# First attention: key blocks of 128 from the first context row on, and a last block of 64 keys for the upper 64 queries

## The reference, cut to what matters

```python
k_full = jnp.concatenate([k_ctx, k], axis=1)
v_full = jnp.concatenate([v_ctx, v], axis=1)
...
causal = jnp.where(j > i, -jnp.inf, 0.0).astype(x.dtype)
mask = jnp.concatenate([jnp.zeros((L, T), x.dtype), causal], axis=1)
scores = jnp.einsum('blhd,bmhd->bhlm', q, k_full) * scale + mask
probs = jax.nn.softmax(scores, axis=-1)
out = jnp.einsum('bhlm,bmhd->blhd', probs, v_full)
...
return out @ wo
```

## Time and profile before

| what | value |
|---|---|
| median of 3 runs | 1954.93 us (1954.01 to 1955.39) |
| span of the profiled execution, first to last instruction | 1951.5 us |
| PE busy | 1834.0 us, 94% |
| DVE busy | 1096.8 us, 56% |
| ACT busy | 1036.9 us, 53% |
| POOL busy | 960.0 us, 49% |
| mean TensorE clock granted | 0.985 of full |

### The profile page before, as it was taken

One profiled execution on the slowest core, in us unless ns is written; L12 is line 12 of the kernel. 1 busy time (PEld: TensorE's weight loads), 2 busy tenths in 40 slices (PEclk: granted clock), 3 DMA queues, 4 the chain that ended last, 5 costly groups with the idle time before them and its releaser, 6 DMA issues. The chain is left out here.

```text
span 1951.5 us, 27620 instructions
## 1 busy us (share of the span) xinstructions
PE 1834.0 (94%) x9759; PEld 1317.1 (67%) x9796; DVE 1096.8 (56%) x2263; ACT 1036.9 (53%) x2248; POOL 960.0 (49%) x864
## 2 busy tenths in 40 slices
PE   7999999999999999999998999989999868869997
PEld 4667666776777666767765877769999646644443
DVE  5554444446445664456545648434343668768886
ACT  3655556655555545554544321126666367757775
POOL 5644455444654445544441100018888455657774
PEclk9999999999999999999999999999999989989999
DMA  7111112111111111011112100147889670000000
GB/s 240 56 51 47 42 35 57 55 32 51 34 40 34 49 55 46 18 34 50 51 65 79 66 22 22 44 136 218 229 235 259 186 162 1 1 1 23 23 17 28
DMA packets 112952, 141.18 MB, mean 72 GB/s; under 512 B 37408, under 2 KB 68128, under 8 KB 112624
## 3 DMA queue, kind: packets, MB, share of 16 engines
q1 hardware_dynamic: 105648, 122.63, 20.1%
q0 software_dynamic: 7168, 16.78, 4.2%
HBM read 104.78 MB, written 29.36 MB: 69 GB/s over the span
## 5 line engine op out<-in xcount | busy, mean ns | idle before, releaser
L750 POOL TENSOR_TENSOR a_xcl<-xT,a_xch 128x512 fp32r<-128x512 f32 x64 | 83.1, 1299 | 317.1 <-ACT a_xch L559 317.1
L909 PE MATMUL a_A<-a_pT,a_vf 128*128 128x512 f32 (+1 forms) x448 | 236.1, 608 | 1.4 <-ACT a_pT L575 1.2
L859 PE MATMUL a_S<-a_kT,a_qT 128*128 128x288 f32 (+3 forms) x640 | 208.8, 424 | 1.7 <-ACT a_pr_odd L565 1.7
L666 DVE TENSOR_REDUCE a_nmax<-a_S 128x1 f32<-128x192 f32 (+3 forms) x256 | 138.1, 551 | 80.5 <-PE a_S L860 79.2
L565 ACT ACTIVATE a_pr_odd<-a_S,a_nmax 128x320 f32<-128x320 f32 (+1 forms) x128 | 81.0, 634 | 152.4 <-DVE a_nmax L666 151.2
L120 PE MATMUL a_A<-a_wlo,a_xch 128*128 128x512 f32 x256 | 151.7, 592 | 2.6 <-DVE a_qT L662 2.6
L575 ACT ACTIVATE a_pT<-a_TR 128x512 f32<-128x512 f32 (+1 forms) x224 | 132.3, 591 | 35.5 <-PE a_TR L899 34.7
L859 PEld LDWEIGHTS a_S<-a_kT,a_qT 128*128 128x128 f32 x640 | 114.7, 189 | 49.6 <-issue 26.8
L1513 POOL TENSOR_TENSOR e_wlo<-expert_raw,e_whi 128x1408 fp32r<-128x1408 f32 x31 | 100.4, 3238 | 67.2 <-ACT e_whi L1685 65.1
L565 ACT ACTIVATE a_pr_even<-a_S,a_nmax 128x192 f32<-128x192 f32 (+1 forms) x128 | 67.1, 526 | 124.8 <-DVE a_nmax L666 124.7
L2429 PE MATMUL f_HH<-w12T,f_f_xqT 128*128 128x512 bf16 x496 | 117.7, 383 | 7.3 <-DVE f_h L2285 4.3
(11 more groups left out here) (393 smaller groups left out, 5178.9 us busy)
## 6 DMA issues: line engine op xcount, KB each, us to landing
a_pw<-in_L_ffn_w_dram SPq DMA_DIRECT2D x96, 256.0 KB, 2.8
expert_raw<-in_L_ffn_w_gate_dram SPq DMA_DIRECT2D x16, 704.0 KB
expert_raw<-in_L_ffn_w_up_dram SPq DMA_DIRECT2D x16, 704.0 KB
expert_raw<-in_L_ffn_w_down_dram SPq DMA_DIRECT2D x16, 512.0 KB
tern<-a_tern SPq DMA_DIRECT2D x48, 128.0 KB, 1.8
x_res<-in_x_dram SPq DMA_DIRECT2D x4, 1024.0 KB, 9.3
a_raw<-in_L_xattn_wq_dram SPq DMA_DIRECT2D x4, 1024.0 KB, 5.5
a_raw<-in_L_xattn_wo_dram SPq DMA_DIRECT2D x4, 1024.0 KB, 5.4
```

The lines of the kernel that those rows point to most:

```text
L666: ve.tensor_reduce(nmax[:, s % 2, i:i + 1], pair(s, i), AX.X, ALU.max, negate=True).then_inc(s_max, 1)
L750: pool.tensor_tensor(xcl[:, t % 2], xT[:, :, tok(t)], xch[:, t % 2].bitcast(F32), ALU.subtract).then_inc(xlo_ready, 1)
L859: pe.matmul(bank[:, lo:hi], qT[:, t % 2, hq], kT[:, par(t), lo:hi], start=True, stop=hi < nk)
L909: last = pe.matmul(A[:, A_USE["V", t, 0][0]], vf[r, par(t), i], pT[r, i % 2], start=i == 0, stop=i == nkt - 1)
```

## The change

Blocks are now counted from the first context row: blocks 0 to b have 128 keys each (block 0: 64 context keys and the first 64 tokens), and the last block, b + 1, has the 64 keys that are left, the upper half of the diagonal block. Under the mask only the upper 64 queries of the tile see them.

- P of the last block turns 64 columns of `pr` per head into 64 rows of the bank.
- g of the last block copies 64 rows and the upper 64 queries of each head, 256 columns, to a buffer of its own, `pT_late`, in 128 rows of which the lower 64 are zeros, set once at the start.
- V of the last block multiplies 128 rows (64 of them zeros) with 256 columns, and adds into the upper 64 queries of each head in the bank. All V now use 128 rows.
- `pT_late` takes the second buffer of `qT`, which has one buffer left.
- `vf` is shifted by 64 rows: tile b's values lie in the lower half of block b and the upper half of block b + 1. The copy on ACT (step v) becomes two copies of 64 rows.
- Before the first V of a tile PE waits for the values of the next tile of the batch also, whose rows the last block reads against zeros; for tile 0 also for the zeros.
- DVE clears 64 rows of the last `vf` block of both buffers at its start, and `pT_late` in slot -1 (step z), behind the turning of the context keys.

```diff
-    ... -1: "v X E A", ...
+    ... -1: "z v X E A", ...
...
-        kc = qT[:].rearrange("p t (h d) -> p t h d", h=KVH)
+        q_and_late = qT
+        kc = q_and_late[:].rearrange("p t (h d) -> p t h d", h=KVH)
+        qT, pT_late = q_and_late[:, 0], q_and_late[:, 1, 0:GH * T]
...
-        def rows(kt):
-            return T if kt == 0 else P
+        def last_block(t, i):
+            return i == t % BT + 1
...
-                        act.activation(pT[0:rows(i), i % 2], TR[0:rows(i), TR_USE["P", t, i][0]], ACT.Copy).then_inc(pT_ready, 1)
+                        bank = TR[:, TR_USE["P", t, i][0]]
+                        if last_block(t, i):
+                            act.activation(pT_late[0:T].rearrange("p (h q) -> p h q", h=GH), bank[0:T].rearrange("p (h q) -> p h q", h=GH)[:, :, T:P],
+                                           ACT.Copy).then_inc(pT_ready, 1)
+                        else:
+                            act.activation(pT[:, i % 2], bank, ACT.Copy).then_inc(pT_ready, 1)
...
-                        act.activation(qT[:, t % 2], TR[:, TR_USE["T", t, 0][0]], ACT.Copy).then_inc(qT_ready, 1)
+                        act.activation(qT, TR[:, TR_USE["T", t, 0][0]], ACT.Copy).then_inc(qT_ready, 1)
...
-                        act.activation(vf[:, par(t), 1 + t % BT], bank[:, HD:2 * HD], ACT.Copy).then_inc(kv_act, 1)
+                        act.activation(vf[T:P, par(t), t % BT], bank[0:T, HD:2 * HD], ACT.Copy)
+                        act.activation(vf[0:T, par(t), t % BT + 1], bank[T:P, HD:2 * HD], ACT.Copy).then_inc(kv_act, 1)
...
+                for u in range(2):
+                    ve.memset(vf[T:P, u, BT], 0.0).then_inc(late_ready, 1)
                 def do(name, i, s, m):
+                    if name == "z":
+                        ve.wait_ge(ck_turned, 2)
+                        ve.memset(pT_late, 0.0).then_inc(late_ready, 1)
...
-                        c0 = 0 if i == 0 else T + P * (i - 1)
                         for h in range(GH):
-                            last = pe.transpose(bank[:, h * P:(h + 1) * P], pr[t % 2][:, h, c0:c0 + P], ident[:])
+                            if last_block(t, i):
+                                last = pe.transpose(bank[0:T, h * P:(h + 1) * P], pr[t % 2][:, h, i * P:i * P + T], ident[:])
+                            else:
+                                last = pe.transpose(bank[:, h * P:(h + 1) * P], pr[t % 2][:, h, i * P:(i + 1) * P], ident[:])
...
-                            until(pe, kv_done, tile, t, m)
+                            until(pe, kv_done, tile, t + 1 if t % BT < BT - 1 else t, m)
+                            if t == 0:
+                                pe.wait_ge(late_ready, 3)
...
-                        r, nkt = slice(0, rows(i)), t % BT + 2
-                        last = pe.matmul(A[:, A_USE["V", t, 0][0]], vf[r, par(t), i], pT[r, i % 2], start=i == 0, stop=i == nkt - 1)
-                        if i == nkt - 1:
-                            last.then_inc(o_full, 1)
+                        bank = A[:, A_USE["V", t, 0][0]]
+                        if last_block(t, i):
+                            pe.matmul(bank.rearrange("p (h q) -> p h q", h=GH)[:, :, T:P], vf[:, par(t), i],
+                                      pT_late.rearrange("p (h q) -> p h q", h=GH), start=False, stop=True).then_inc(o_full, 1)
+                        else:
+                            pe.matmul(bank, vf[:, par(t), i], pT[:, i % 2], start=i == 0, stop=False)
```

More of the change, by code:

```diff
@@ L154, in attention0_stage @@
     DVE_SLOT = "M0 M1 N0 L D X v M2 N1 N2 j0 j1 M3 N3 B E A"
-    DVE_ORDER = {"last": "A0 A1 X0 D X1 r0 A2 X2 r1 A3 X3 r2 r3 B", -3: "A0 A1 X0 A2 X1 A3 X2 X3 b u c0 t0 c1 t1", -2: "v A E", -1: "v X E A", "first": DVE_SLOT,
+    DVE_ORDER = {"last": "A0 A1 X0 D X1 r0 A2 X2 r1 A3 X3 r2 r3 B", -3: "A0 A1 X0 A2 X1 A3 X2 X3 b u c0 t0 c1 t1", -2: "v A E", -1: "z v X E A", "first": DVE_SLOT,
                  0: DVE_SLOT, 1: DVE_SLOT, 2: "M0 M1 N0 L D X v M2 N1 N2 j0 M3 N3 j1 B E A", 3: DVE_SLOT}
@@ L328, in attention0_stage @@
         kw_loaded = s_.sem("kw_loaded")
+        late_ready = s_.sem("late_ready")
         ident_loaded, causal_loaded, gates_loaded, tri_loaded = (s_.sem(n) for n in ("ident_loaded", "causal_loaded", "gates_loaded", "tri_loaded"))
@@ L858, in do @@
                         for lo, hi in pieces:
-                            pe.matmul(bank[:, lo:hi], qT[:, t % 2, hq], kT[:, par(t), lo:hi], start=True, stop=hi < nk)
+                            pe.matmul(bank[:, lo:hi], qT[:, hq], kT[:, par(t), lo:hi], start=True, stop=hi < nk)
                         pe.matmul(bank[:, nk - P:nk], ident_b[:], causal[:], start=False, stop=True).then_inc(s_full, 1)
```

## The result

The changed kernel takes 1920.2 us (median of 4, 1918.46 to 1922.39) where the kernel before takes 1955.16 us beside it. The ratio is 0.9825, with a 95% interval of 0.9811 to 0.9839: 35 us faster, of 47 us forecast. Kernel before and changed kernel are 1951.5 and 1916.6 us long in their profiled executions, so these show the same 35 us.

The account below looks back on a forecast made before the run. The prediction took PE's queue to bound the first attention. From the profiled 1951.5 us it took off 53.1 (25.6 + 27.5), added 6.4 of give-backs and 3.4 from profile to median: 1908 us, range 1898 to 1936.

Parts of the forecast that it names:

- first term: PE around V0: value blocks of 128 keys avoid going to 64 array rows and back, 0.40 us a slot, 25.6 us.
- second term: PE's last value block: 256 columns instead of 512 save 0.43 us in each of 64 slots, 27.5 us.
- slots without room: Slots that also convert weights on ACT and POOL: five keep today's length, giving back 4 us.
- second value copy and what waits behind it: ACT's added copy, 0.18 us, delays v, M2, e2, g1; V1 stalls in two kinds of slot, 2.4 and 1 us.
- PE's prices: PE: excursion 0.40 us, 256-column pass 0.215 us, four 64-wide transposes 0.60 us, strided output at no cost.
- strided output: Rival on PE's last value matmul: its strided output streams like 512 columns, 27.5 us more, 1936; chance 0.05.
- column mode: Rival on PE's 64-wide transposes: the array's column mode costs what its row mode does, 25.6 us more, 1934; chance 0.10.
- transposes without their one-pass form: Rival on PE: 64-wide transposes become ordinary two-pass f32 matmuls, 1.24 us a slot, 79 us, 1987; chance 0.05.
- two side terms: PE's wait for the last block's copy goes, 3 us gained; the next output projection W0 waits, 2 us lost.
- ACT and the waits: Prediction's part on ACT's copies and PE's resulting waits: give-backs of 6.4 us, bounds -3 and 16.
- The rival that put 12 us more on this chain: Value copies, v, M2, e2, g1, V1 hold PE up 0.25 us in the 48 other slots too, 1920; chance 0.12.
- sign of being wrong: In PE's changed profile: 64-wide transposes spread, 256-column passes start 0.4 us apart, or stage idle time passes 20 us.

Follow-up runs that it names:

- e5: Kernel before with only its context block of 64 keys filled up to 128 rows with zeros; one value copy, last block whole: 1937.7 us.
- e6: Changed kernel with the last block again copied and multiplied on all 512 columns instead of 256, its transposes still 64 wide: 1950.0 us.
- e1: Changed kernel with one value copy of 128 rows to the old place instead of two of 64 rows (values not right): 1908.0 us.
- e2: Changed kernel with DVE's third maximum M2 ahead of step v in every slot: 1909.8 us.
- e3: Kernel before with DVE's third maximum M2 ahead of step v: 1953.6 us. Beside M3, the name means ACT's exponential step instead.
- e4: Changed kernel with DVE's two ternary pieces moved behind M3 and the last probability scaling, in slots of kind 1 (b = 1) only: 1917.3 us.
- e7: Changed kernel with M2 ahead of v except in kind 2 (b = 2), and the two ternary pieces of kind 1 placed apart: 1904.3 us.
- e9: Kernel before with its context block padded to 128 rows, as in e5, plus M2 ahead of v on DVE: 1940.6 us.
- e8: Changed kernel with both value copies of 64 rows kept, each to the rows it comes from, not shifted (output differs): 1913.4 us.
- e10: Changed kernel as in e7, with the ternary pieces split in slots of kinds 0 and 3 (b = 0, 3) too: 1916.3 us.

## Why the prediction was right, and where it was not

The four measurements e5, e6, the changed kernel and e1 split the 35 us by the prediction's own steps. The first term alone is e5. The changed kernel without the second term is e6, so e6 less e5 is the price of the copies, and the changed kernel less e6 the second term; e1 gives the copies' price a second time.

| step | forecast, us | measured, us |
|---|---|---|
| (1) no excursion to 64 rows | -25.6, less 4 in slots without room | -15.9 (e5) |
| second value copy and what waits behind it | +3.4 | +12.3 (e6 - e5), +11.6 (changed - e1) |
| (2) 256 columns, T's and W0's waits | -27.5 - 3 + 2 | -30.6 (changed - e6) |
| sum | -46.7 | -34.2 |

e5 has the 1.0 us of its own slot 0; without it the first two rows are -16.9 and +13.3. The single query buffer, the 64-wide transposes and V0's wait for the next tile's values were not run alone. e6 - e5 holds them and changed - e1 does not, so they cost 0.7 us (1.7 without slot 0), no more than the intervals allow.

**PE's prices held.** 0.39 us around V0 for 0.40, 0.22 us a pass of 256 columns for 0.215, 0.60 us for the four 64-wide transposes, no price for the strided output; ACT's narrower copy took 0.36 us for the 0.38 estimated. So the three rivals on PE (column mode 1934, strided output 1936, transposes without their one-pass form 1987) fall. The Trainium skill (TensorEngine Tiling (Array Packing), Key Properties) has a drain at each change of mode; the trace agrees with 0.39 us for 64 rows and shows nothing of it for 64 columns. Its Restrictions have the f32 transpose mode among what column tiling disables; nothing of that shows here, as the 64-wide transposes run 0.109 us apart like the full ones.

**The second term held**, with its two side terms: T's wait went (e6 puts a size on it), W0's came (1.8 us).

**The step that failed is "ACT and the waits", in two of its terms.** The value copies were priced at 0.18 us from two operations that begin at the same partition; they start 0.28 us apart, so that the last ends 611.88 - 611.04 = 0.84 us behind the square's start, where it was 0.45 (662.65 + 0.27 - 662.47 in the earlier trace rows). That is 0.39 us, not 0.18. (V1's room was taken too small, which goes the other way: V1 starts 0.05 us behind the copy that it waits for, not 0.14.) And I followed it to one reader only, V1 in two kinds of slot. There the mechanism was right and the size was not: V1 waits for g1 in every slot of kinds 0 and 3, and that costs 0.23 us a slot in kind 3 for 0.15 and 0.20 in kind 0 for less than 0.1, 5.6 us in the 26 of them behind the early slots, for 3.4 in all. The chain has two more readers, as behind e2 ACT also has the copy of the turned tokens, which P1 waits for, and behind N2 DVE has the ternary pieces, M3, e3 and with them the queries of the next slot.

The rival that put 12 us more on this chain came to the measured time partly by luck. e1 and e2 show that the chain is real, as they move it by 12 and 10 us. But the rival's 12 stood on top of the 3.4, the copies cost 12 in all, and the rest of the missing gain lies in the slots without room. It also let the chain reach PE by V1 in every slot; in kinds 1 and 2 V1 starts 0.48 us or more behind g1's end, and what PE meets there is the first scores and P1. (In kind 1 g1 is the slot's last copy and stands behind e2 on ACT, not behind e3 as was said above of all kinds.)

**The other term is the slots without room**, "if five of them keep today's length". There are 15, not five, and 13 of them keep their length without the copies too (e5). The slack of 0.15 us in the ternary slots stands in the trace of before; I had read the ends of waits only in the slot of the earlier trace rows and in none with ternary pieces. A mean over 720 us says that PE is the bound nearly everywhere, and hides that in a quarter of the slots something else sets the end, or nearly does.

One sign of being wrong that the prediction named was met: from the start of slot 0 to that of slot 63 PE is idle for 21.5 us (13.2 before), just past the 20 named. The other two, spreading transposes and 256-column passes 0.4 us apart, were not.

What stays open: whether the ternary slots of kind 1 give their 0.40 us in the kernel of e5 once the pieces are moved was not run. In the changed kernel e4 and e7 show that they do; in e9, by its trace, what M2 gained there was lost where the piece met POOL.

## What to carry to other kernels

An engine that is busy 99% of the time still has slots in which a second chain ends just behind it: before a saving is multiplied by the number of slots, measure the slack (the operand's end to the waiting instruction's start) in one slot of every class, and pay the saving only up to it. Read waits from these two times and not from idle time alone, which showed nothing of V1's. Follow a delayed signal through everything queued behind its waiter, on each engine in turn, and price an operation from a row with the same neighbours: the same start partitions on ACT, the same company on POOL. After PE has been made quicker, try the order strings again; a reorder that was worth nothing was worth 10 us, and with the pieces of one kind split and kind 2 left as it was, 15.

## What the hardware showed that was not expected

- In the square and the value copies ACT starts an operation 0.10 us before the one ahead ends (0.17 us apart with 0.28 and 0.27 us of duration) where input and output begin at the same partitions as that one's. Where the output, or both, begin at another, it starts 0.01 us after that end (0.28 us apart). This held in 64 of 64 slots of the changed kernel and of e8, medians -104 ns against +11 and +12 ns from end to start. The Trainium skill (ScalarE: Activation LUTs, What ACT_TABLE_LOAD costs) says that ACTIVATEs back to back overlap by some 93 ns; the trace agrees where the partitions stay, and not where they move.
- DVE's two ternary operations took 0.48 and 0.75 us with POOL idle, and in e10, with POOL working, 1.39 to 1.43 and 1.51 to 1.63 us. Their ends (590.89 and 592.55 in the rows of e10) lie 0.29 and 0.55 us behind the end of the POOL operation that they met (590.60 and 592.00), and in the row of e9 the first one's lies 0.28 us behind (625.57, 625.29), so they look blocked by it and not slowed. The Trainium skill (SBUF — State Buffer, Who interferes with whom) has this as an exclusive lock of a port pair that the two engines share; these ends agree with it.
- Transposes that load 64 columns cost PE neither more nor less than full ones (0.109 us each), while going to 64 rows and back costs 0.39 us.
